# Hybrid attention and expert block: the five instruction orders written anew, and the row maxima's DMA issued by ScalarE

## The chip, the cores and the metric

One core of one Trainium2 chip. The metric is the device time of one execution in microseconds (us), lower is better. The kernel before took 746.04 us in the median of 3 runs (742.22 to 750.68).

## The reference, cut to what matters

The input is 8 sequences of 256 rows of 512 numbers in float32. Two rounds are computed on it, the second on the first one's result; each is an attention followed by an expert layer, both with a residual.

```
x = x + attention(layernorm(x))   # 32 heads of 16, 8 key/value heads, RoPE, causal softmax
x = x + experts(layernorm(x))     # dense 512x512 + bias, and the top 2 of 8 low-rank experts (rank 16)
x = x + attention_b(layernorm(x)) # same shapes, other weights
x = x + experts(layernorm(x))
```

Everything is float32 in value. The kernel makes the matrix products exact enough by splitting each operand into a high part (rounded to fp32r) and a low part (what is left), and adding three products.

## The kernel before, in words

**Stages.** A sequence in one round is a *slot* `s`; there are 16 of them, 0 to 15. A slot's attention is cut into four steps `p` = 4s to 4s+3 (64 in all) and two *halves* `h` = 2s and 2s+1 (32 in all). For a slot, TensorE (PE) runs, by the helper's name in the code:

- `tr("a")`: transposes of the normalised rows; `q01` and `q2`: projections for queries, keys and values, 8 steps each (12 and 6 matmuls a step); `vT`: transposes of the values.
- for each `p`: `A` (three pieces, all scores once, only to find each row's maximum), `M2` (transposes of those maxima), `B` (three pieces, the scores again with the maximum subtracted, through extra rows of the operand that hold the maxima), and for each half `PV` (probabilities times values, with the row sums).
- `oM`: output projection, 8 steps of 6 matmuls. Steps 0 and 1 of its four row blocks read half 2s, steps 2 and 3 read half 2s+1.
- `tr("f")`, `fA`, `fB`, `fW`, `fC`: the expert layer (router and low-rank inputs, dense product, transposes, low-rank outputs).

**The way of the maxima.** VectorE (DVE) reduces the scores (`Am`, L1094), PE transposes (`M2`, L507), ScalarE (ACT) copies them to a row tile (`mc`, to `mT`, L860), and a DMA of 8 KB (`mr`, L293) writes them into the operand tile `QK` of that step. `B` (L517) waits for it, then ACT takes the exponential (`ex`, L940), and GpSimd (POOL) masks (`causal`, L1259). There is one `mT`: `mc(p)` waits until `mr(p-1)` has landed.

**The way of the operands.** ACT copies the projections out of PSUM (`qe`, L860), SyncE (SP) swaps odd and even rows by DMA (`sw`, L270), DVE and POOL rotate (`rc`, `rs_`, `ra`), ACT and POOL split into high and low (`rh`, `kh`, `rl`, `kl`), and SP lays them out for the four steps by 12 DMAs (`st`, L282 to L287). The first rotation of the next slot (`rc`) waits until all 12 have landed. `A` of a step waits for its three.

**The way of the row sums.** After `PV(h)`: ACT copies (`oe`, L860), a DMA gathers the sums (`lc`, L299), DVE inverts (`rp`, L1123), two more transfers through DRAM spread them (`rd`, L308; `rr`, L314), `xc` (L303) moves the numerators, POOL or DVE multiplies (`mu`, L235), ACT and POOL split (`oh`, L860; `ol`, L246). Then `oM` may read.

**The way to the expert layer.** After `oM`: DVE adds the residual (`ox`, L1137), takes statistics (L1079), ACT and POOL make the scale (`eps`, L895; `power`, L1248), ACT normalises twice (`norm`, L902), PE transposes, ACT and DVE split (`high`, L860; `low`, L1064). Then `fA` may start. At the end of a slot `fx` (L1179) adds the result and SP stores it.

**Order.** Nothing chooses at run time. Each of the five engines has its own list of calls, written out in the source by a planner that ran before; the engines meet at semaphores only, and each engine works strictly in the order of its list. A step that is not ready holds up all that stands behind it on its engine, and SP's list holds all DMAs. The last argument of a PE call, as `("ex", 171)`, is the semaphore that frees its PSUM buffer.

Of the kernel before, what the change touches and what calls it, by code (L numbers as in the profile page):

```python
# [5 lines left out]
F32 = mybir.dt.float32  # L6
# [6 lines left out]
P = 128  # L13
# [42 lines left out]
def hybrid_block_kernel(nc, x_in, wqa, woa, wqb, wob, wg, wb, wl, bias_in, trig_in, krow_in, iden_in, iota_in, sums,  # L56
                        mid, out):
    with ExitStack() as ctx:
# [198 lines left out]
        def _(e):  # L257
# [146 lines left out]
            rr(27); lc(28); xc(28); st(62, 2); st(62, 0); st(62, 1); rd(28); mr(60); rr(28); st(63, 1); st(63, 0)
            st(63, 2); store(12); mr(61); lc(29); mr(62); xc(29); rd(29); rr(29); mr(63); lc(30); xc(30); rd(30)
            lc(31); rr(30); xc(31); rd(31); rr(31); store(13); store(14); store(15)
# [4 lines left out]
        def _(e):  # L411
# [175 lines left out]
            warm(5); tr("a", 0, 0); tr("a", 1, 0); q01(0, 0, 0, 1); q2(0, 0, 0, 2); q01(0, 0, 1, 1); q01(0, 1, 1, 1)  # L587
            q2(0, 0, 1, 2); q01(0, 1, 0, 1); q01(0, 2, 0, 1); q01(0, 3, 0, 1); q2(0, 1, 1, 2); q01(0, 2, 1, 1)
            q01(0, 3, 1, 1); q2(0, 1, 0, 2); q2(0, 2, 0, 2); q2(0, 3, 0, 2); q2(0, 2, 1, 2); q2(0, 3, 1, 2); vT(0, 3)
            tr("a", 2, 0, ("al", 1)); tr("a", 3, 0); q01(1, 0, 0, 1, ("rc01", 1)); q01(1, 1, 0, 1); q01(1, 2, 0, 1)  # L590
            q01(1, 3, 0, 1); q2(1, 0, 0, 2, ("rc2", 1)); q01(1, 0, 1, 1); q01(1, 1, 1, 1); q01(1, 2, 1, 1)
            q01(1, 3, 1, 1); q2(1, 1, 0, 2); q2(1, 2, 0, 2); q2(1, 3, 0, 2); q2(1, 0, 1, 2); q2(1, 1, 1, 2)
            q2(1, 2, 1, 2); q2(1, 3, 1, 2); A(0, 0, 3, ("ve", 1)); vT(1, 0, ("al", 2)); A(0, 1, 0, ("ve", 2))
            A(0, 2, 3, ("m", 1)); A(1, 0, 1, ("rc01", 2)); A(1, 1, 2, ("rc2", 2)); A(1, 2, 0, ("m", 2))
            M2(0, 3, ("m", 3)); A(2, 0, 3, ("mc", 1)); A(2, 1, 1, ("m", 4)); A(2, 2, 2, ("m", 5)); M2(1, 0, ("m", 6))
            B(0, 0, 0, ("mc", 2)); B(0, 1, 3, ("m", 7)); B(0, 2, 0, ("ex", 1)); tr("a", 4, 3, ("ex", 2))
            B(1, 0, 1, ("m", 8)); B(1, 1, 0, ("ex", 3)); M2(2, 2, ("m", 9)); B(1, 2, 1, ("ex", 4))
            A(3, 0, 2, ("mc", 3)); A(3, 1, 0, ("ex", 5)); A(3, 2, 2, ("m", 10)); B(2, 0, 1, ("ex", 6)); tr("a", 5, 3)
            A(4, 0, 0, ("m", 11)); PV(0, 1, ("ex", 7)); M2(3, 2, ("m", 12)); A(4, 1, 0, ("m", 13))
            q01(2, 0, 0, 3, ("al", 3)); q01(2, 1, 0, 3); A(4, 2, 1, ("oe", 1)); B(2, 1, 2, ("mc", 4))  # L600
            B(2, 2, 0, ("m", 14)); q01(2, 2, 0, 3); q01(2, 3, 0, 3); M2(4, 1, ("m", 15)); B(3, 0, 2, ("ex", 8))
            q01(2, 0, 1, 3); B(3, 1, 0, ("ex", 9)); B(3, 2, 1, ("mc", 5)); q01(2, 1, 1, 3); q01(2, 2, 1, 3)
# [826 lines left out]
```

## Time and profile before

| | |
|---|---|
| median of 3 runs | 746.04 us |
| the profiled execution | 747.37 us |
| its span, first to last instruction | 745.4 us |
| mean granted TensorE clock | 0.937 of full speed |
| PE busy | 662.7 us (89%) |
| DVE, ACT, POOL busy | 458.7, 433.4, 469.6 us |
| DMA | 95.14 MB, mean 128 GB/s |

PE matmuls overlap and their ends are modelled, so the busy share of PE is not its share of peak. Waits are given for the engine that waited and the one that released it. A granted clock of 0.5 is the lower of the two levels, 1.2 GHz; 1.0 is 2.4 GHz.

### The profile page before, as it was taken

Reading aid. Unit: us, or ns where it says so; the run is one execution under the profiler, and the core shown is the slowest. Engines: PE = TensorE matmul, PEld = TensorE weight load, DVE = VectorE, ACT = ScalarE, POOL = GpSimd, SP = SyncE. Lnnn points to the kernel's source line nnn. Section 1 sums busy time; section 2 is a strip of 40 time slices with the busy share of each in tenths; the row PEclk is TensorE's granted clock in tenths of the full one; section 3 lists DMA queues with packets and bytes.
Section 4 is the critical chain, followed back from the end, with each engine's and each line's share of the span. In section 5 each row is a group of like instructions: output and inputs, shape, how many; then the busy total and the mean of one; then the engine's idle time right before and its main releaser. Section 6 shows DMA issues by size and latency. Waiting matters only on the chain.

```text
span 745.4 us, 18400 instructions
## 1 busy us (share of the span) xinstructions
PE 662.7 (89%) x7498; PEld 508.1 (68%) x7498; DVE 458.7 (62%) x641; ACT 433.4 (58%) x698; POOL 469.6 (63%) x494
## 2 busy tenths in 40 slices
PE   5675989998999998998999899999999799698896
PEld 4663556876677776776777687777776687464684
DVE  2677464765576766765675765767676654664543
ACT  2535556655565766756575674848576465556531
POOL 1337295857677684957677584958676665855531
PEclk7775889999999999999999899999999899899999
DMA  9563536353464646364454626464644626264111
GB/s 324 171 192 61 115 99 150 76 140 103 100 180 100 183 103 175 99 178 136 104 176 100 203 66 153 128 130 138 137 140 106 149 76 148 90 126 108 49 37 57
DMA packets 49651, 95.14 MB, mean 128 GB/s; under 512 B 7936, under 2 KB 19840, under 8 KB 49568
## 3 DMA queue, kind: packets, MB, share of 16 engines
q1 hardware_dynamic: 49568, 93.98, 47.9%
q8 instruction: 59, 0.97, 0.5%
q14 instruction: 24, 0.20, 0.1%
HBM read 24.42 MB, written 10.49 MB: 47 GB/s over the span
## 4 chain that ended last, share of the span: by engine, by line
PE 55%; DMA 13%; SPq 11%; POOL 6%; issue 6%; ACT 5%; DVE 4%; POOLq 0%; DVEq 0%; ACTq 0%
PE PP L424 38%; PE PP L531 10%; PE PP L517 5%; DMA NR<-sums 2%; SPq L314 2%; SPq L285 2%; DMA Qs<-Qf 2%; SPq L282 2%; DMA QK<-R 2%; DMA QK<-mT 2%; ACT PT L940 2%; SPq L287 2%; PE PP L437 2%; DVE nm L1094 1%; POOL PT L1259 1%
## 5 line engine op out<-in xcount | busy, mean ns | idle before, releaser
L1094 DVE TENSOR_REDUCE nm<-PP 128x4 f32<-128x1024 f32 (+1 forms) x192 | 227.8, 1217 | 89.9 <-PE PP L424 89.3
L940 ACT ACTIVATE PT<-PP 128x1024 f32<-128x1024 f32 x192 | 191.6, 1024 | 66.9 <-PE PP L517 65.7
L1259 POOL TENSOR_SCALAR_AFFINE_SELECT PT<-PT 128x1024 f32<-128x1024 f32 x128 | 139.4, 1095 | 111.4 <-ACT PT L940 111.4
L424 PE MATMUL PP<-QK 64*128 64x128 f32 (+1 forms) x1024 | 97.0, 296 | 17.9 <-ACT PT L940 3.9
L531 PE MATMUL PP<-PT,V 128*32 128x512 f32 x768 | 95.7, 634 | 13.8 <-POOL PT L1259 11.1
L424 PE MATMUL PP<-XH,WQh 64*128 64x256 f32 x768 | 99.9, 308 | 7.9 <-DVE XL L1064 4.8
L424 PEld LDWEIGHTS PP<-QK 64*128 64x128 f32 x1024 | 83.6, 201 | 31.7 <-issue 13.7
L424 PE MATMUL PP<-XL,WQh 64*128 64x256 f32 x768 | 92.7, 290 | 0.0
L424 PE MATMUL PP<-XH,WQl 64*128 64x256 f32 x768 | 92.6, 289 | 0.0
L517 PE MATMUL PP<-QK 64*128 64x512 f32 x384 | 82.2, 435 | 10.5 <-DMA QK<-mT 5.0
L424 PEld LDWEIGHTS PP<-XH,WQh 64*128 64x128 f32 x768 | 70.4, 199 | 21.0 <-issue 12.0
L424 PEld LDWEIGHTS PP<-XL,WQh 64*128 64x128 f32 x768 | 69.2, 198 | 1.0
L204 POOL TENSOR_TENSOR Qs<-Qs,trig 128x512 f32<-128x512 f32 (+1 forms) x46 | 51.0, 1117 | 28.8 <-DMA Qs<-Qf 28.6
L424 PEld LDWEIGHTS PP<-XH,WQl 64*128 64x128 f32 x768 | 69.1, 197 | 0.0
L531 PEld LDWEIGHTS PP<-PT,V 128*32 128x32 f32 x768 | 23.2, 114 | 63.9 <-issue 50.5
L235 POOL TENSOR_TENSOR NE<-NE,NR 128x512 f32<-128x512 f32 x30 | 38.4, 1278 | 43.2 <-DMA NR<-sums 43.2
L902 ACT ACTIVATE xn<-X,nb,rs 128x512 f32<-128x512 f32 x64 | 51.9, 812 | 18.2 <-POOL nb L1250 11.4
L860 ACT ACTIVATE NE<-PP 128x1024 f32<-128x1024 f32 x32 | 32.8, 1025 | 49.8 <-PE PP L531 49.7
L424 PE MATMUL PP<-WOh,OH 64*128 64x512 f32 x256 | 56.0, 426 | 2.2 <-POOL OL L246 1.9
L424 PE MATMUL PP<-WBh,XH 64*128 64x512 f32 x256 | 55.3, 421 | 0.9 <-DVE nm L1094 0.4
L1248 POOL TENSOR_TENSOR rs<-ve,half 128x2 f32<-128x2 f32 x32 | 22.6, 707 | 51.8 <-ACT nme L896 51.6
L517 PEld LDWEIGHTS PP<-QK 64*128 64x128 f32 x384 | 38.6, 194 | 22.6 <-DMA QK<-mT 7.1
(95 smaller groups left out, 1302.7 us busy)
## 6 DMA issues: line engine op xcount, KB each, us to landing
QK<-Rh SPq DMA_DIRECT2D x64, 256.0 KB, 4.1
QK<-R SPq DMA_DIRECT2D x64, 208.0 KB, 4.1
QK<-R SPq DMA_DIRECT2D x64, 160.0 KB, 4.0
Qs<-Qf SPq DMA_DIRECT2D x32, 256.0 KB, 3.3
NR<-sums SPq DMA_DIRECT2D x64, 128.0 KB, 2.7
NE<-NE SPq DMA_DIRECT2D x32, 128.0 KB, 2.0
mid<-X SPq DMA_DIRECT2D x8, 512.0 KB, 5.0
X<-mid SPq DMA_DIRECT2D x8, 512.0 KB, 4.6
```

Of the source, the lines that this page charges most:

```text
L204: e.tensor_tensor(schunk(b), schunk(b), trigs(1, b), ALU.mult).then_inc(S[f"rs{b}"], 1)
L235: e.tensor_tensor(n, n, NR[:, :], ALU.mult).then_inc(S["mu"], 1)
L282: e.dma_start(QK[0:P:2, g, 0:1024].bitcast(F32), Rh[rows, :, :].rearrange("r c t -> r (c t)").unsqueeze(1).to_broadcast([32, 2, 1024]).bit ...
L424: ins = e.matmul(t[:, k, c], lhs(rows, which[k]), rhs(rows, which[k]), start=start, stop=stop, skip_group_check=True)
L517: ins = e.matmul(PP[t][:, a, :].rearrange("p (j q) -> p j q", j=4), keys(g, a, 4 if i == 2 else 0), x[:, :, min(i, 1), :], start=True, sto ...
L531: ins = e.matmul(PP[t][32 * c:32 * c + 32, min(i, 1), :], V[:, s % 2, i // 2, 4 * G + c, :], PT[:, (3 * p + i) % RING, 512 * a:512 * a + 5 ...
L860: return e.activation(dst, src, ACT.Copy)
L902: e.activation(xn[:, f, :], X[:, 2 * (s % XR) + i, :], ACT.Identity, bias=nb[:, f, i:i + 1], scale=rs[:, f, i:i + 1]).then_inc(S[c + "xn"], 1)
L940: e.activation(PT[:, k % RING, :].rearrange("p (a x) -> p a x", a=2), PP[t][:, :, :], ACT.Exp, scale=0.25).then_inc(S["ex"], 1)
L1094: e.tensor_reduce(o, x, AX.X, ALU.max).then_inc(S["m"], 1)
L1248: e.tensor_tensor(rs[:, f, :], ve_[:, f, :], half[:, :], ALU.pow).then_inc(S["np" + c], 1)
L1259: e.affine_select(out=blk, in_=blk, compare_op=ALU.is_ge, fill=0.0, base=0, pattern=[[0, 8], [1, 128]], channel_multiplier=-1).then_inc(S[ ...
```

## The change

It has two parts. The amount of work is the same on each engine, but for the 64 `mr` DMAs and 7 more warm-up matmuls at PE's start.

**1. `mr` is issued by ACT.** The function moves from the block of SP to that of ACT, and in ACT's list `mr(p)` always stands right behind `mc(p)`.

**2. All five lists are written anew.** In SP's list the opening loads stand in the order in which they are used (rows, then the four blocks of the first projection's weights, then the rest), where before they were mixed. In all lists the steps of attention and expert layer interleave otherwise. Which engine does a step is unchanged; the PSUM buffers are assigned anew.

```diff
             # block of SP
-            def mr(p):
-                w.wait_ge(S["mc"], p + 1)
-                e.dma_start(QK[3:P:64, p % 4, 0:1024].bitcast(F32),
-                            mT[:, :].bitcast(F32)).then_inc(S[f"md{p % 2}"], 16)
...
-            rows0(0); load(0); rows0(1); load(13); const("id"); load(6); load(14); load(5); load(16); kr(); load(7)
-            const("trig"); load(3); load(2); rows(1); rows(2); load(1); load(15); load(10); const("bias"); rows(3)
-            const("iota"); load(12); load(8); load(11); load(4); rows(4); load(9); qk(); sw(0, 0); sw(0, 2); st(0, 0)
-            st(1, 0); st(2, 0); st(3, 0); st(0, 1); st(1, 1); st(2, 1); st(0, 2); st(1, 2); st(3, 1); st(2, 2)
-            st(3, 2); sw(1, 0); sw(1, 2); wd(17); mr(0); mr(1); st(4, 0); st(4, 2); st(4, 1); mr(2); st(5, 2)
+            rows0(0); rows0(1); const("id"); load(0); load(1); load(2); load(3); const("trig"); rows(1); kr()
+            load(4); load(5); load(6); load(7); qk(); load(12); load(13); load(14); load(15); load(16); load(8)
+            load(9); load(10); load(11); rows(2); const("bias"); const("iota"); rows(3); rows(4); sw(0, 0); sw(0, 2)
+            wd(17); st(0, 0); st(1, 0); st(2, 0); st(3, 0); st(0, 2); st(1, 2); st(2, 2); st(3, 2); st(0, 1)
+            st(1, 1); st(2, 1); st(3, 1); sw(1, 0); sw(1, 2); st(4, 0); st(4, 2); st(4, 1); st(5, 1); st(5, 0)
...
             # block of PE, a slot in the middle of the run (after)
+            PV(22, 0, ("ex", 138)); B(46, 2, 2, ("ex", 139)); A(47, 1, 1, ("ex", 140)); A(47, 2, 3, ("ox", 11))
+            q01(13, 0, 0, 0, ("oe", 23)); q01(13, 1, 0, 0); q01(13, 2, 0, 0); q01(13, 3, 0, 0); M2(47, 1, ("m", 143))
+            tr("f", 20, 2, ("ex", 141)); A(48, 0, 3, ("m", 144)); A(48, 1, 1, ("mc", 48)); q01(13, 0, 1, 0)
+            q01(13, 1, 1, 0); tr("f", 21, 2); B(47, 0, 3, ("m", 145)); q01(13, 2, 1, 0); B(47, 1, 1, ("m", 146))
+            q01(13, 3, 1, 0); B(47, 2, 3, ("ex", 142)); fA(10, 0, 0, 2, ("fl", 11)); fA(10, 1, 0, 2); fA(10, 2, 0, 2)
...
             # block of ACT
+            def mr(p):
+                w.wait_ge(S["mc"], p + 1)
+                e.dma_start(QK[3:P:64, p % 4, 0:1024].bitcast(F32),
+                            mT[:, :].bitcast(F32)).then_inc(S[f"md{p % 2}"], 16)
...
             # block of POOL, opening
-            power("a", 0); power("a", 1); rs_(0, 1); ra(0, 1); ra(0, 2); rl(0, 1); kl(0); rs_(1, 0); rs_(1, 2)
+            power("a", 0); power("a", 1); ra(0, 2); rs_(0, 1); ra(0, 1); power("a", 2); kl(0); rl(0, 1)
```

## Rows read from the trace of the kernel before

**Rows 1.** The page: busy time of the engines, clock in 40 slices.

```profile
PE 662.7 (89%) x7498; PEld 508.1 (68%) x7498; DVE 458.7 (62%) x641; ACT 433.4 (58%) x698; POOL 469.6 (63%) x494
PEclk7775889999999999999999899999999899899999
```

**Rows 2.** By stretch: length, busy PE, PEld, DVE, ACT, POOL; PEclk, DMA, GB/s.

```profile
0.00:80.00 80.00, 51.71 (x482) 40.71 (x484) 45.30 (x62) 34.66 (x61) 29.89 (x35) 0.70 0.59 177
80.00:151.30 71.30, 64.34 (x740) 49.81 (x741) 41.65 (x48) 43.76 (x65) 50.33 (x49) 0.93 0.51 118
151.30:568.40 417.10, 392.25 (x4679) 304.94 (x4677) 278.42 (x388) 266.84 (x428) 296.24 (x311) 0.98 0.52 135
568.40:695.00 126.60, 110.39 (x1172) 79.67 (x1172) 71.70 (x93) 72.92 (x111) 77.95 (x80) 0.93 0.44 109
695.00:745.40 50.40, 44.03 (x444) 33.02 (x444) 21.61 (x52) 15.19 (x35) 15.19 (x22) 0.98 0.15 53
```

**Rows 3.** Chain that ended last, opening (start us, length us, what).

```profile
8.50 9.72 DMA PT<-in_wqa
...
20.13 6.86 PE PP L424 x70
...
28.65 2.43 DMA Qs<-Qf
...
35.84 0.59 SPq L282
```

**Rows 4.** Timeline, opening: first projection, next rotation, `mr` issues, first `B`.

```profile
14.79 0.58 PE L424 MATMUL PP<-XH,WQh 64*128 64x256 f32 x2 [2.47 <-DVE XL L1064]
...
51.28 1.22 DVE L1103 TENSOR_TENSOR R<-PP,trig 128x1024 f32<-128x1024 f32 x1 [2.43 <-DMA QK<-R]
...
60.13 4.85 SPq L293 DMA_DIRECT2D QK<-mT  x2
...
64.53 1.22 PE L517 MATMUL PP<-QK 64*128 64x512 f32 x4 [2.09 <-ACT mT L860]
```

**Rows 5.** `mr`: issue durations (min/median/max ns), and waits (us, times, longest).

```profile
L293 SPq DMA_DIRECT2D QK<-mT x64: 535/580/846, 60.1 to 686.1; - x64
...
PEld PP L517 <- DMA QK<-mT: 7.1, 10, 3.2
...
PE PP L517 <- DMA QK<-mT: 5.0, 6, 3.0
...
SPq L293 <- ACT mT L860: 35.7, 21, 9.4
```

**Rows 6.** Chain of waits: PE's steps at full clock (start, us, what).

```profile
261.24 0.23 PE PP L517 x2
...
263.15 0.72 PE PP L424 x12
...
707.91 3.06 PE PP L424 x24
```

**Rows 7.** Timelines of PE, POOL and DVE: half 9 in mid-run, half 31 last.

```profile
254.52 2.78 PE L531 MATMUL PP<-PT,V 128*32 128x512 f32 x24 [1.67 <-POOL PT L1259]
...
277.97 1.28 POOL L246 TENSOR_TENSOR OL<-NE,OH 128x512 fp32r<-128x512 f32 x1 [0.74 <-ACT OH L860]
...
694.96 2.78 PE L531 MATMUL PP<-PT,V 128*32 128x512 f32 x24
...
710.79 0.69 DVE L246 TENSOR_TENSOR OL<-NE,OH 128x512 fp32r<-128x512 f32 x1 [0.54 <-ACT OH L860]
```

**Rows 8.** Timeline of DVE: residual (`ox`) and low part (`low`), slot 3, slot 15.

```profile
244.16 1.22 DVE L1137 TENSOR_TENSOR X<-PP,X 128x1024 f32<-128x1024 f32 x1 [0.39 <-PE PP L424]
...
256.79 1.22 DVE L1064 TENSOR_TENSOR XL<-PP,XH 128x1024 fp32r<-128x1024 f32 x1
...
719.34 1.22 DVE L1137 TENSOR_TENSOR X<-PP,X 128x1024 f32<-128x1024 f32 x1
...
728.49 1.23 DVE L1064 TENSOR_TENSOR XL<-PP,XH 128x1024 fp32r<-128x1024 f32 x1 [0.73 <-ACT XH L860]
```

More of the change, by code:

```diff
@@ L585, in fC @@
                 ins.then_inc(S["fC"], 1)
[L587 to L600, printed above, removed]
@@ L852, in _ @@
-            fB(15, 1, 0, 0); fB(15, 2, 0, 0); fB(15, 3, 0, 0); fB(15, 0, 1, 0); fB(15, 1, 1, 0); fB(15, 2, 1, 0)
-            fB(15, 3, 1, 0); fW(15, 2, ("fl", 16)); fC(15, 1, 0); fC(15, 0, 0)
+            warm(7); tr("a", 0, 0); warm(1); tr("a", 1, 0); warm(4); q01(0, 0, 0, 1); q2(0, 0, 0, 2); q01(0, 0, 1, 1)
+            q01(0, 1, 1, 1); q01(0, 1, 0, 1); q2(0, 0, 1, 2); q2(0, 1, 1, 2); q01(0, 2, 0, 1); q01(0, 3, 0, 1)
+            q01(0, 2, 1, 1); q01(0, 3, 1, 1); tr("a", 2, 3); q2(0, 1, 0, 2); q2(0, 2, 0, 2); q2(0, 3, 0, 2)
@@ new lines, in _ @@
+            M2(0, 3, ("m", 2)); B(0, 0, 0, ("m", 3)); B(0, 1, 1, ("rc2", 2)); A(1, 0, 3, ("mc", 1))
+            A(1, 1, 2, ("rc01", 2)); A(1, 2, 0, ("ex", 1)); A(2, 0, 3, ("m", 4)); A(2, 1, 1, ("ex", 2))
+            M2(1, 2, ("m", 5)); B(0, 2, 0, ("m", 6)); A(2, 2, 2, ("mc", 2)); A(3, 0, 3, ("m", 7))
+            A(3, 1, 1, ("m", 8)); M2(2, 0, ("ex", 3)); A(3, 2, 2, ("m", 9)); B(1, 0, 0, ("mc", 3))
+            B(1, 1, 3, ("m", 10)); B(1, 2, 0, ("ex", 4)); q01(2, 0, 0, 1, ("m", 11)); q01(2, 1, 0, 1)
@@ new lines, in _ @@
+            B(7, 1, 0, ("ex", 22)); B(7, 2, 1, ("m", 25)); q01(3, 3, 1, 2); A(8, 1, 3, ("fl", 1))
+            fA(0, 0, 0, 0, ("ex", 23)); fA(0, 1, 0, 0); fA(0, 2, 0, 0); fA(0, 3, 0, 0); fA(0, 0, 1, 0)
+            fA(0, 1, 1, 0); fA(0, 2, 1, 0); fA(0, 3, 1, 0); A(8, 2, 1, ("ex", 24)); PV(3, 3, ("m", 26))
+            fB(0, 0, 0, 0, ("fg", 1)); fB(0, 1, 0, 0); fB(0, 2, 0, 0); fB(0, 3, 0, 0); M2(8, 1, ("m", 27))
+            fW(0, 3, ("oe", 4)); A(9, 0, 2, ("rc01", 4)); fB(0, 0, 1, 0); fB(0, 1, 1, 0); fB(0, 2, 1, 0)
@@ new lines, in _ @@
+            B(37, 0, 0, ("mc", 39)); B(37, 1, 2, ("m", 118)); oM(8, 2, 1, 3); oM(8, 3, 1, 3)
+            B(37, 2, 0, ("ex", 112)); A(39, 1, 1, ("al", 12)); oM(8, 2, 0, 3); oM(8, 3, 0, 3)
+            B(38, 0, 2, ("ex", 113)); B(38, 1, 0, ("ex", 114)); PV(18, 1, ("m", 119)); A(39, 2, 3, ("ox", 9))
+            B(38, 2, 2, ("ex", 115)); q01(11, 0, 0, 0, ("ex", 116)); q01(11, 1, 0, 0); M2(39, 1, ("oe", 19))
+            q01(11, 2, 0, 0); q01(11, 3, 0, 0); tr("f", 16, 3, ("m", 120)); q01(11, 0, 1, 0)
@@ new lines, in _ @@
+            M2(51, 0, ("oe", 25)); q01(14, 3, 0, 1); tr("f", 22, 2, ("m", 156)); q01(14, 0, 1, 1)
+            A(52, 0, 3, ("ex", 153)); A(52, 1, 0, ("mc", 52)); tr("f", 23, 2); q01(14, 1, 1, 1)
+            B(51, 0, 3, ("m", 157)); q01(14, 2, 1, 1); q01(14, 3, 1, 1); B(51, 1, 0, ("m", 158))
+            B(51, 2, 3, ("ex", 154)); fA(11, 0, 0, 2, ("fl", 12)); fA(11, 1, 0, 2); fA(11, 2, 0, 2); fA(11, 3, 0, 2)
+            A(52, 2, 0, ("ex", 155)); fA(11, 0, 1, 2); fA(11, 1, 1, 2); fA(11, 2, 1, 2); fA(11, 3, 1, 2)
@@ new lines, in _ @@
+            split(8); split(9); split(10); rs_(0, 0); ra(0, 0); rs_(0, 2); low("a", 1, 3); stats("a", 2); split(11)
+            stats("a", 3); stats("a", 4); rl(0, 0); low("a", 2, 0); Am(0, 0, 0); Am(0, 1, 3); Am(0, 2, 0)
+            rc(1, 2, 1); rc(1, 0, 2); Am(1, 0, 3); Am(1, 1, 2); Am(1, 2, 0); Am(2, 0, 3); Am(2, 1, 1); Am(2, 2, 2)
+            Am(3, 0, 3); Am(3, 1, 1); Am(3, 2, 2); rp(0); Am(4, 0, 0); Am(4, 1, 3); Am(4, 2, 2); Am(5, 0, 0)
+            rc(2, 0, 1); Am(5, 1, 2); rp(1); rc(2, 2, 0); Am(5, 2, 0); Am(6, 0, 2); Am(6, 1, 1); low("a", 3, 3)
```

920 lines of the change are left out of this document (451 added, 469 removed).

## The prediction

> **What bounds the kernel now.** The page first: PE is busy 662.7 us of a span of 745.4, no other engine over 63% [rows 1]. So PE sets the pace, and what a new order can win is what PE idles, 83 us, and what it runs at the lower clock. Where that lies, a table by stretch shows [rows 2]: until 80 us PE is busy 51.7 us at a granted clock of 0.70; from 80 to 151.3 (the `PV` of half 4) 64.3 of 71.3 at 0.93; the 20 halves up to 568.4 take 417.1 us, of which PE works 392.3 at 0.98, 20.9 us a half or 41.7 a slot; 568.4 to 695.0 has 110.4 of 126.6 at 0.93; the tail after the last `PV`, 44.0 of 50.4. Idle time: 28 us in the first 80, 7 in the next 71, 25 in the long middle, 16 late, 6 in the tail.
>
> The chain of waits tells what the opening waits for: a weight load of 9.7 us that ends at 18.2, half clocked PE work to 27, the swap until 31.1, rotation, then twelve `st` from 35.8 [rows 3]. The first `B` comes at 64.53, behind two `mr` issues that together held SP's queue 4.85 us [rows 4].
>
> **Part 1: `mr` on ACT.** It takes 64 issues of 0.58 us off SP, 37 us, with the 35.7 us in which SP stood at them for `mc`, and with that held up swaps, layouts and row sum transfers queued behind. It adds the 64 issues to ACT. From 0.535 (the shortest) to 0.846 us (the longest) each [rows 5] that is 34 to 54 us; I take 0.58 plus about 0.2 in which ACT waits for the end of its own copy (an estimate; the rows do not show that gap), 50 us. ACT goes from 433 to 483 us, 65% of the span, still below PE. What PE ever waited for `mT`'s transfer is 7.1 + 5.0 = 12.1 us [rows 5]: that is the upper bound of a gain. The lower bound is that all 50 us delay something PE needs: behind `mr` on ACT stand exponentials, copies for the projections, `oe` and `oh`. Each has slack of several us in most places, as ACT idled over 40%. Cover of the cost: that idle time. If it is gone, the exponentials come late, and PE's B and PV wait. I take −3 for `mr` and +3 for late ACT work, net 0, ends −12 and +51.
>
> A wait is not added beyond what was there: `mr(p)` behind `mc(p)`; `mc(p+1)` waits for the landing of `mr(p)` as before. SP's transfers and ACT's no longer pass one queue. The Trainium skill (DMA: Bandwidth & Descriptors, "Issuing engines are not separate DMA queues") says that issuing on several engines only saves the issue time; the zero above agrees. The same notes (Perfetto Trace Analysis, "DMA Instruction — HWDGE (DVE, Sync)") have the issuing sequencers share one descriptor generator with a lock wait ahead of it, which speaks against the change: ACT would stand while SP issues. No row of before shows ACT issuing, so the sum goes without it; it is a rival below.
>
> **Part 2a: the opening.** Rows and first weights now lead the queue. PE starts at 14.79 at the lower clock, and its first projection ends at 20.13 + 6.86 = 27.0 [rows 3, 4]. With the four weight blocks one behind another it should end around 22, 5 us sooner. But all of it does not carry through: the layouts need rotation, all weight splits and `wd(17)` ahead of `st`, and the remaining loads (some 8 MB) still run. So `st` starts only 0 to 1.5 us sooner than 35.84. The other gain is in PE's list: `B` of the first step now stands ahead of further `A`s, so it should come around 54 in place of 64.53, and with it exponentials, `PV` and the next projections. Not all 10.5 us count, as PE then meets less work that is ready. Seven more warm-up matmuls cost under 1 us and lie in PE's idle time before its first weights. Bounds at the `PV` of half 4 (151.3): −1.5 from `st` alone to −11 from `B` alone; I take −7.
>
> **Part 2b: the middle.** PE's work is the same: by steps of 0.72 (`q01`), 0.77 (a quarter of 3.06 for an `oM`, `fB` or `fC` step), 0.23 (`B`), 2.78 (`PV`) [rows 6, 7] a slot comes to some 36 to 37 us, against 41.7 now. A gain of up to 4 to 5 us a slot is there, if the waits go. But the new order sets two waits tighter. Counting PE work by these prices in both lists: between `PV` of the odd half and the third step of `oM` there were 21.1 us, now 15.5; from the end of `oM` to `fA` 15.0, now 11.2. What these must cover: from `PV`'s end to `ol`'s end 279.25 − 257.30 = 21.9 us in mid-run and 711.48 − 697.74 = 13.7 at the end with the queues empty [rows 7]; from `ox` to `low`, 258.0 − 244.2 = 13.9 and 729.7 − 719.3 = 10.4 [rows 8]. One slot then cannot be shorter than the first chain, 4 `oM` steps and 2 `B` (3.5), the second chain, and 8 `fA`, 2 `fB`, an `A` and a `PV` (6.5; an `fA` or `A` is 4 matmuls of 0.06, from twelve in 0.72): 24.1 + 10.0 = 34.1 with the short chains, 35.8 + 10.0 = 45.8 with the long. Even with now is at chains of 31.7. Both long chains contain POOL time that depends on the list: in half 9 `ol` alone began at 277.97, behind rotations of the next slot, and in POOL's new list `mu` of the odd half stands ahead of a rotation (`rs_`, `ra`), a `kl` and two masks that were ahead of it; SP has less in its way too. I take 29, a loop of 39, for PE a slot hardly shorter than it was once its own work and small waits are in, and +3 over the ten slots for places where a cover fails. Ends: −24 (2.4 a slot, half of what PE idles per slot, as 39.3 would be) and +41 (45.8 each slot).
>
> **Part 2c: late and tail.** 16 us idle in 126.6, at 0.93 [rows 2]: before, the last slots left PE less to mix. The new lists interleave slots 14 and 15 as the middle does; at the middle's busy share of 94%, 110.4 would take 117, −9; that is one end, +3 the other, and I take −6. In the tail PE has less work behind the last `PV` (no first half of `oM` left over) but also less filler under the 13.7 us of its chain [rows 7]; the whole tail is nearly that chain, the second one and the expert layer: −2, between −5 and +3.
>
> **Sum.** 745.4 − 7 + 0 + 3 − 6 − 2 = 733.4 us span. The profiled execution stands 2.0 over its span, at 747.4, and 1.3 above the median: 733.4 + 2.0 − 1.3 = 734.
>
> **Rivals.**
> *Nothing net (745, between 739 and 752).* The covers fail by 1 us a slot (+10), the opening gives −7 and the late stretch −3. For it: PE's idle time in the middle is only 25 us already, and every lost wait uncovers another. Against: the opening's order is a plain mistake repaired, and nothing there competes with it.
> *Slower: `ol` comes too late (762).* If POOL and ACT serve the row sums as in half 9, the loop is 45.8; if that holds in seven slots of ten, 7 × 4.1 = +29, and with −7 −6 for opening and end, the span is 761 to 762. It decides where the two chains sum to over 31.7 us; the wait is PE's third `oM` step on `OL`, and its price 45.8 − 41.7 = 4.1 a slot at most. ACT's issues make it likelier, as `oe` and `oh` lie in the first chain and two `norm`s in the second: half a us more for each of two or three `mr` passed is +1.5 a slot. Against: ACT and SP share the load better.
> *A shared issue path.* If ACT's issue has to wait until one of SP's is through, each `mr` costs ACT one SP issue more, 64 × 0.58 = 37 us [rows 5], and ACT comes to 520 us, still under PE. What of it falls in the chains above, two `mr` a slot, is 1.2 us a slot: 12 in the middle and some more around it, 747. For it: two `mr` issues of SP once took 4.85 us together [rows 4], so an issue can be held up by something. Against: the longest single one took 0.846. It is the lock wait of the Trainium skill, as above.
> *More gain (718).* The middle gives −12 and the opening −11.
> *The change does nothing in time* cannot quite be: both parts reach every list; it falls in the first rival.
>
> **Chances.** Forecast 0.5 (its own range 722 to 741), nothing net 0.19, a shared issue path 0.05, slower 0.21, more gain 0.05. Range 718 to 760: the case of more gain at the lower end, and the slower case in its milder half. A measurement of this kernel tells about 1% from no change, 738.6 to 753.5. Faster by over that: 0.52; within: 0.26; slower: 0.22.
>
> **What would show it.** The first projection over by 23 and first `B` near 54; the `PV` of half 4 near 144. If `B` comes at 60 or later, 2a is wrong. From half 4 to half 24, 417 us again within 5; if longer, PE's waits name POOL `OL` (first chain) or DVE `XL` and ACT `xn` (second), and these sums over 25 us mean the slower rival. ACT issues of `mr` at 0.6 us, and SP's waits on `mT` gone; ACT issues of over 1 us mean that SP and ACT get in each other's way. From half 24 to 31 about 120 us, and a tail of 48. What would make me wrong altogether: a queue whose turn order I misjudged, as POOL's rotation of a next slot ahead of `mu`, which repeats in every slot.

## The result and the profile after

In 20 runs each, the changed kernel took 747.13 us in the median (742.24 to 751.86) and the kernel before 744.93 us (735.53 to 751.96). The ratio is 1.0053 (95% interval 1.0029 to 1.0077): half a per cent slower, where 734 us and a gain were forecast.

The page of the changed kernel: busy times, and the clock in 40 slices. They answer to [rows 1].

```profile
PE 662.0 (89%) x7512; PEld 503.4 (67%) x7512; DVE 453.7 (61%) x641; ACT 432.0 (58%) x698; POOL 469.4 (63%) x494
...
PEclk9785999999999999999999999999999999997999
```

PE has the same busy time in the same span. The clock rose from 0.937 to 0.952 on the mean, and only its second to fourth slices and one near 680 us are low.

The table by stretch, cut at the `PV` of halves 4, 24 and 31 as in [rows 2] (the cut at 80 us is a fixed time):

```profile
0.00:80.00 80.00, 49.95 (x512) 41.06 (x516) 41.94 (x60) 35.05 (x62) 27.20 (x35) 0.77 0.66 177
80.00:153.70 73.70, 66.59 (x766) 49.91 (x758) 43.33 (x53) 45.99 (x69) 53.09 (x53) 0.98 0.50 123
153.70:575.70 422.00, 395.53 (x4686) 306.01 (x4684) 275.51 (x386) 264.62 (x427) 297.28 (x310) 0.99 0.52 133
575.70:699.30 123.60, 110.97 (x1166) 77.38 (x1166) 72.41 (x93) 73.42 (x112) 78.97 (x81) 0.93 0.44 108
699.30:746.10 46.80, 38.95 (x392) 29.04 (x392) 20.49 (x51) 12.90 (x32) 12.88 (x19) 0.97 0.15 52
```

| until | before | after | difference | forecast |
|---|---|---|---|---|
| `PV` of half 4 | 151.3 | 153.7 | +2.4 | −7 |
| half 4 to 24 | 417.1 | 422.0 | +4.9 | +3 |
| half 24 to 31 | 126.6 | 123.6 | −3.0 | −6 |
| tail | 50.4 | 46.8 | −3.6 | −2 |
| sum | 745.4 | 746.1 | +0.7 | −12 |

Of the 12.7 us between forecast and result the opening makes 9.4. Its chain of waits, beside [rows 3]:

```profile
5.26 8.72 DMA NE<-in_krow
14.00 0.77 SPq L355
14.81 0.58 SPq L329
15.44 3.86 SPq L329
19.35 3.28 SPq L329
...
28.00 0.70 SPq L270
28.74 7.08 DMA Qs<-Qf
35.84 0.70 DVE Qs L204
...
42.43 0.59 SPq L282
```

The weights were in time: PE's first projection ended at 19.5, not at 27. But SP stood until 14.0 at `qk` (L355, a broadcast of 832 KB into `QK`), because it copies what `kr` (L350, 208 KB into `NE`) brings, and `kr` landed only then. After it two single load issues took 3.86 and 3.28 us. The first swap (L270) was issued at 28.00, as before, although its data were ready at 20.5, and its transfer took 7.08 us where it took 2.43 [rows 3]. The loads that went out late were still under way then: from 28 to 30 us the DMA engines were 97% busy, before 37%. So `st` began at 42.43, in place of 35.84. These 6.6 us have two parts. The last transfer of the first swaps landed at 36.15, before at 32.20, which is 4.0 us. From there to `st`, with rotation and split between, it was 6.3 us, before 3.6: 2.6 us that lie in rotation and split, whose order on DVE and POOL is new as well. PE stood too, for 10.4 us until 38.85, at a projection of slot 1: its operand `XL` stands behind a rotation of slot 0 in DVE's list, and that rotation waited for the swap.

ACT's issue of `mr`, and who waits for `mT` (beside [rows 5]):

```profile
L923 ACTq DMA_DIRECT2D QK<-mT x64: 503/518/1122, 58.6 to 688.8; - x64
...
PEld PP L508 <- DMA QK<-mT: 10.5, 8, 2.4
...
PE PP L508 <- DMA QK<-mT: 5.9, 5, 2.2
```

An issue costs 0.52 us on ACT in the median, 33 us in all, and only one took 1.12. In the trace each begins 0.03 us behind the end of its copy, and ACT's next instruction starts at least 0.59 us behind that end.

### The profile page after: what moved, and what is told of

Read it like the earlier page. It is cut to its first block, busy times and chain, and to the rows that moved or that the text cites. A ratio compares the mean times of both kernels' runs of the same rounds, so it can differ in the third digit from the quotient of the medians.

```text
span 746.1 us, 18427 instructions
## 1 busy us (share of the span) xinstructions
PE 662.0 (89%) x7512; PEld 503.4 (67%) x7512; DVE 453.7 (61%) x641; ACT 432.0 (58%) x698; POOL 469.4 (63%) x494
## 4 chain that ended last, share of the span: by engine, by line
PE 55%; DMA 12%; SPq 8%; ACT 8%; DVE 7%; POOL 4%; issue 4%; ACTq 0%; DVEq 0%; POOLq 0%
PE PP L415 40%; PE PP L522 9%; PE PP L508 4%; DVE nm L1094 4%; DMA Lc<-NE 4%; ACT PT L935 3%; DMA Qs<-Qf 3%; SPq L282 2%; PE PP L428 2%; SPq L287 2%; SPq L329 2%; ACT NE L850 2%; DMA QK<-R 1%; SPq L285 1%; DMA NE<-in_krow 1%
## 5 line engine op out<-in xcount | busy, mean ns | idle before, releaser
L1094 DVE TENSOR_REDUCE nm<-PP 128x4 f32<-128x1024 f32 (+1 forms) x192 | 227.3, 1216 | 69.1 <-PE PP L415 68.4
L935 ACT ACTIVATE PT<-PP 128x1024 f32<-128x1024 f32 x192 | 188.1, 1025 | 61.2 <-PE PP L508 58.1
L415 PE MATMUL PP<-XH,WQh 64*128 64x256 f32 x768 | 94.9, 296 | 12.5 <-DVE XL L1064 11.0
L415 PE MATMUL PP<-QK 64*128 64x128 f32 (+1 forms) x1024 | 92.8, 295 | 11.5 <-DVE nm L1094 4.2
L415 PEld LDWEIGHTS PP<-QK 64*128 64x128 f32 x1024 | 77.7, 196 | 33.5 <-issue 17.3
L508 PE MATMUL PP<-QK 64*128 64x512 f32 x384 | 77.9, 432 | 15.4 <-DMA QK<-mT 5.9
L415 PE MATMUL PP<-XL,WQh 64*128 64x256 f32 x768 | 90.1, 283 | 0.0
L415 PE MATMUL PP<-XH,WQl 64*128 64x256 f32 x768 | 90.0, 283 | 0.0
L204 POOL TENSOR_TENSOR Qs<-Qs,trig 128x512 f32<-128x512 f32 (+1 forms) x46 | 50.9, 1108 | 33.2 <-DMA Qs<-Qf 33.1
L209 POOL TENSOR_TENSOR R<-R,Qs 128x512 f32<-128x512 f32 (+1 forms) x47 | 51.6, 1100 | 26.1 <-DVE Qs L204 21.1
L415 PEld LDWEIGHTS PP<-XL,WQh 64*128 64x128 f32 x768 | 66.3, 191 | 0.8
L1123 DVE RECIPROCAL Lc<-Lc 128x128 f32<-128x128 f32 x32 | 30.4, 950 | 51.8 <-DMA Lc<-NE 51.7
L508 PEld LDWEIGHTS PP<-QK 64*128 64x128 f32 x384 | 37.1, 190 | 31.5 <-DMA QK<-mT 10.5
```

Of the source, the lines that this page charges most:

```text
L204: e.tensor_tensor(schunk(b), schunk(b), trigs(1, b), ALU.mult).then_inc(S[f"rs{b}"], 1)
L209: e.tensor_tensor(roped(b), roped(b), schunk(b), ALU.add).then_inc(S[f"ra{b}"], 1)
L415: ins = e.matmul(t[:, k, c], lhs(rows, which[k]), rhs(rows, which[k]), start=start, stop=stop, skip_group_check=True)
L508: ins = e.matmul(PP[t][:, a, :].rearrange("p (j q) -> p j q", j=4), keys(g, a, 4 if i == 2 else 0), x[:, :, min(i, 1), :], start=True, sto ...
L935: e.activation(PT[:, k % RING, :].rearrange("p (a x) -> p a x", a=2), PP[t][:, :, :], ACT.Exp, scale=0.25).then_inc(S["ex"], 1)
L1094: e.tensor_reduce(o, x, AX.X, ALU.max).then_inc(S["m"], 1)
```

## The experiments

Twelve kernels ran, in three sets; the ratios of a set are to the kernel before, run beside them.

**1. The place of `mr`, the place of `qk`, the loads.**

`e1_mr_sp`: the new lists, `mr` back on SP.

```diff
-            mc(0, 3); mr(0); ...          # ACT
+            mc(0, 3); ...
-            sw(1, 0); sw(1, 2); st(4, 0); st(4, 2); st(4, 1); ...      # SP
+            sw(1, 0); sw(1, 2); mr(0); mr(1); st(4, 0); st(4, 2); mr(2); st(4, 1); ...
```

> The new lists, but the 64 mr go back to SP's list, each at the place in the order of start times that it had in the profiled run of the changed kernel. Theory A (mr on ACT neither costs nor gains, as I forecast; the missing gain lies in the opening): within 0.5% of the changed kernel, 743 to 751 us. Rival B (mr on ACT costs ACT time that PE then misses: 50 us in all, of which some 5 to 10 reach the end): 737 to 742. Rival C (mr on ACT is worth something, since SP's queue is full, and it hides a loss of the new order): 751 to 758.

Measured: 747.1 us, ratio 1.0015 (0.9979 to 1.0051). Theory A's range holds it. Against the 1.0053 of the changed kernel it is 0.4% less, which the intervals do not tell from nothing. The waits of PE for `mT` went up from 10.5 and 5.9 to 16.7 and 11.1 us, and the span is no longer for it (745.6 against 746.1).

`e2_mr_act`: the old lists, only `mr` moved.

```diff
-            sw(1, 0); sw(1, 2); wd(17); mr(0); mr(1); st(4, 0)         # SP
+            sw(1, 0); sw(1, 2); wd(17); st(4, 0)
-            mc(0, 3); eps("a", 3); mc(1, 0); ...                       # ACT
+            mc(0, 3); mr(0); eps("a", 3); mc(1, 0); mr(1); ...
```

> The lists of the kernel before, with only the 64 mr moved from SP's list to ACT's, each right behind its mc. Theory A: within 0.5% of the kernel before. Rival B: slower by 5 to 10 us. Rival C: faster by 3 to 7 us. The profile tells what an mr costs on ACT (0.6 us forecast) and whether ACT stands behind SP's issues (over 1 us each).

Measured: 744.4 us, ratio 0.9965 (0.9930 to 0.9999), in A's range and near the edge of C. PE's waits for `mT` almost disappear, from 7.1 and 5.0 us [rows 5]:

```profile
PEld PP L509 <- DMA QK<-mT: 1.5, 2, 0.8
...
PE PP L509 <- DMA QK<-mT: 1.1, 2, 0.6
```

`e3_qk_late`: the changed kernel, with `qk` late.

```diff
-            load(4); load(5); load(6); load(7); qk(); load(12); ...; rows(3); rows(4); sw(0, 0); sw(0, 2)
+            load(4); load(5); load(6); load(7); load(12); ...; rows(3); rows(4); sw(0, 0); qk(); sw(0, 2)
```

> The changed kernel, with one DMA moved in SP's opening: qk (832 KB to QK) from behind the eighth weight load to behind the first swap. Theory A (in the changed kernel SP waited 5.7 us for kr before qk, and qk's 10 us transfer then held the loads, so that the first swap was issued at 28.0 and landed at 35.8): the last loads land by about 20, the first swap lands by 27 to 30, st(0,0) starts at 35 to 37 in place of 42.4, the PV of half 4 comes 4 to 7 us sooner than 153.7; if the opening carries through to the end, 740 to 743 us. Rival D (what the opening wins is lost before the end, since each slot's chain sets the pace): st as much sooner, but 745 to 748 us in all. Rival E (qk's place is harmless): st(0,0) again at 41 to 43.

Measured: 743.7 us, ratio 0.9945 (0.9910 to 0.9979), 1.1% under the changed kernel's ratio, by one DMA's place in a list of 416 entries. The timeline of SP's queue:

```profile
21.23 0.56 SPq L270 DMA_DIRECT2D Qs<-Qf  x1
...
22.46 0.71 SPq L355 DMA_DIRECT2D QK<-NE  x1
24.49 0.50 SPq L270 DMA_DIRECT2D Qs<-Qf  x1
25.03 4.78 SPq L271 DMA_DIRECT2D Qs<-Qf  x1
...
38.45 3.93 SPq L282 DMA_DIRECT2D QK<-Rh  x4
```

The first swap goes out 6.8 us sooner. The second stands behind `qk`, and one of its issues takes 4.78 us. `st` starts at 38.45, the `PV` of half 4 at 147.4 in place of 153.7, and the span ends 5.6 us sooner. Theory A was right in the mechanism: the first swap landed by 27.4. `st` is 1.5 us later than its range, for the second swap, which landed at 33.2, and the median is 0.7 us above its 740 to 743. D fails: what the opening wins does reach the end.

`e4_loads`: the old lists, only the opening loads in the order of use.

```diff
-            rows0(0); load(0); rows0(1); load(13); const("id"); load(6); load(14); load(5); load(16); kr(); ...
-            ...; rows(4); load(9); qk(); sw(0, 0); sw(0, 2); st(0, 0)
+            rows0(0); rows0(1); const("id"); load(0); load(1); load(2); load(3); const("trig"); rows(1); kr(); ...
+            ...; rows(3); rows(4); qk(); sw(0, 0); sw(0, 2); st(0, 0)
```

> The kernel before, with only its opening loads put in the order of use (rows, the four blocks of the first projection's weights, then the others as in the changed kernel), qk last ahead of the first swap as it was. Theory A: q01 of slot 0 is over by 21 in place of 27.0, but the first swap still stands behind qk; it lands at 29 to 31; st(0,0) starts at 33 to 35.8, and the time is 0 to 3 us under the kernel before. Rival D: st sooner by some us and no difference in all. Rival E (loads in the order of use hold up what ACT and DVE do next): st(0,0) after 37, slower by 1 to 5 us.

Measured: 747.7 us, ratio 1.0018 (0.9981 to 1.0054). No difference in all, as D had it, but not on D's way: `st`, which D had sooner, came at 36.61, 0.8 us later than in the kernel before and between the ranges of A and E. SP's queue shows why:

```profile
15.84 0.48 SPq L340 DMA_DIRECT2D X<-in_x  x1
16.37 1.16 SPq L360 DMA_DIRECT2D QK<-NE  x1
23.20 0.54 SPq L270 DMA_DIRECT2D Qs<-Qf  x1
23.79 5.30 SPq L271 DMA_DIRECT2D Qs<-Qf  x1
...
36.61 3.90 SPq L282 DMA_DIRECT2D QK<-Rh  x4
```

The swap is issued 4.9 us sooner than in the kernel before and ends no sooner, as `qk` (here L360) is ahead of it: `qk` landed at 30.6, the swap's transfers at 30.8 and 31.9 (before 30.4 and 31.1). Sooner weights alone are worth nothing. The run also parts the two reasons for the early first projection. With the loads in order and the old warm-up it ended at 22.1, as forecast, with a granted clock of 0.50 from 10 to 18 us and 22 matmuls in 2 us from 14 to 16 and from 16 to 18. The changed kernel, with seven more warm-up matmuls, has a clock of 1.00 and 33 to 34 matmuls there, and ends it at 19.5.

**2. The opening, taken apart.**

`e5_qk_last`: `qk` behind both swaps, else the changed kernel.

```diff
-            ...; load(7); qk(); load(12); ...; rows(4); sw(0, 0); sw(0, 2)
+            ...; load(7); load(12); ...; rows(4); sw(0, 0); sw(0, 2); qk()
```

> The changed kernel with qk behind both first swaps (the run before it had qk between them, and the second swap, issued at 24.5, waited for its data until 33). Theory A (transfers pass in the order of issue, and qk's 10 us stand in the way of what comes behind): the second swap lands by 30, ra(0,2) starts by 31 in place of 33.8, st(0,0) starts at 35 to 37 in place of 38.4, and the time is 1 to 3 us under that run, 0.990 to 0.994 of the kernel before. Rival F (st must then wait for qk itself): st(0,0) at 36 or later with its wait on NE, no gain over that run.

Measured: 741.5 us, ratio 0.9948 (0.9910 to 0.9986).

```profile
24.33 0.60 SPq L271 DMA_DIRECT2D Qs<-Qf  x1
24.97 0.72 SPq L355 DMA_DIRECT2D QK<-NE  x1
...
34.79 4.00 SPq L282 DMA_DIRECT2D QK<-Rh  x4
```

The issue of 4.78 us is gone, the second swap landed at 28.5, `st` starts 3.7 us sooner, slightly sooner than theory A's range, and `PV` of half 4 is at 146.1. In time A's gain over the run before, 1 to 3 us, is missing: the ratio is the same and just outside A's 0.990 to 0.994, the profiled span, 741.7, is no shorter than the 740.5 of the run before, and the `PV` of half 8 came at 237.5 against 236.4. F's sign, `st` at 36 or later with its wait on `NE`, did not come: `st` followed the split of `Rh`, which ended at 34.70. But `qk`, for which `st` waits as well, had landed only at 34.54, so that an earlier rotation alone would win next to nothing. And the first swap took 7.0 us here too, with no `qk` ahead of it.

`e6_kr_first`: only `kr` moved forward, `qk` in its place.

```diff
-            rows0(0); rows0(1); const("id"); load(0); ...; rows(1); kr()
+            rows0(0); rows0(1); kr(); const("id"); load(0); ...; rows(1)
```

> The changed kernel with only kr moved, from the tenth to the third place of SP's list; qk stays behind the eighth weight load. It parts the two halves of the theory on the opening. If SP's wait for kr (5.7 us) was the cost, that wait is gone, the first swap is issued at 23 to 25 in place of 28.0, and 3 to 5 us are gained, 0.998 to 1.001 of the kernel before. If the transfer of qk is the cost, the loads behind it are held as before, the first swap is issued at 26 to 28, and the ratio stays at 1.003 to 1.007.

Measured: 743.2 us, ratio 1.0010 (0.9980 to 1.0039). The timeline of SP:

```profile
12.73 4.73 SPq L329 DMA_DIRECT2D PT<-in_wl  x1
17.50 3.58 SPq L329 DMA_DIRECT2D Wst<-in_wg  x4
...
23.57 1.02 SPq L270 DMA_DIRECT2D Qs<-Qf  x1
...
38.40 4.53 SPq L282 DMA_DIRECT2D QK<-Rh  x4
```

The swap is issued at 23.57, 4.4 us sooner, and the span is 3.1 us shorter; a load issue of 4.73 us behind `qk` stays. The ratio is at the upper edge of the 0.998 to 1.001 expected for the wait. So the wait for `kr` and the place of `qk` each had a share: with the wait gone the `PV` of half 4 came at 150.7, 3.0 us sooner, and with `qk` late 6.3 and 7.6 us sooner.

`e7_open`: the whole opening.

```diff
-            qe(0, 0, 1); norm("a", 3); wh(12); wh(13); wh(14); wh(15); qe(0, 2, 2)      # ACT
+            qe(0, 0, 1); norm("a", 3); qe(0, 2, 2); wh(12); wh(13); wh(14); wh(15)
-            rc(0, 0, 1); split(12); split(13); split(14); split(15); rc(0, 2, 2)        # DVE
+            rc(0, 0, 1); rc(0, 2, 2); split(12); split(13); split(14); split(15)
-            power("a", 0); power("a", 1); ra(0, 2); rs_(0, 1); ra(0, 1)                 # POOL
+            power("a", 0); power("a", 1); rs_(0, 1); ra(0, 1); ra(0, 2)
```

with SP's list as in `e5_qk_last`.

> The changed kernel with its whole opening in the order in which results are there: qk behind both swaps, on ACT the copy qe(0,2) ahead of the splits of the fourth weight group, on DVE rc(0,2) likewise, on POOL rs_(0,1) and ra(0,1) ahead of ra(0,2). Theory A: st(0,0) at 33 to 36 in place of 42.4, the PV of half 0 by 71, the end 8 to 11 us sooner than the changed kernel, 0.989 to 0.993 of the kernel before. Rival G (st needs all thirteen weight copies and qk, and these end no sooner): st(0,0) at 37 or later, 0.993 to 0.996.

Measured: 742.9 us, ratio 0.9971 (0.9936 to 1.0005). Its `st` starts at 35.59, the `PV` of half 0 at 70.3 and of half 4 at 144.4, and the profiled span is 737.5, 8.6 us under the changed kernel's. By the trace A holds. By the ratio it does not in this set: 0.9971 is above A's 0.989 to 0.993 and above G's range too. The edits on ACT, DVE and POOL are not shown to add anything to `qk`'s new place: `st` is 0.8 us later than in `e5_qk_last`, whose ratio in the same set is 0.9948. It was run once more below.

`e8_old_open`: the old lists with `mr` on ACT and this opening on SP.

```diff
-            ...; rows(4); load(9); qk(); sw(0, 0); sw(0, 2); ...; wd(17); mr(0); mr(1); st(4, 0)
+            ...; rows(3); rows(4); sw(0, 0); sw(0, 2); qk(); ...; wd(17); st(4, 0)
```

> The lists of the kernel before with mr on ACT, the opening loads in the order of use and qk behind both first swaps. It tells whether the new interleaving is worth anything beside an opening that is as good. Theory H (old and new interleaving are worth the same, the parts that count are mr on ACT and the opening): 0.991 to 0.995 of the kernel before, as the best of the new lists. Rival I (the new interleaving is better by some us up to its late stretch): 0.994 to 0.999.

Measured: 743.2 us, ratio 0.9960 (0.9922 to 0.9999). The ratio lies in I's range and just above H's, and its interval overlaps both. I does not follow from it: `e5_qk_last`, the new lists with the same place of `qk`, has 0.9948 in the same set, 0.1% less. The new interleaving is not shown to be worth anything beside the old one with an opening as good; nor is the opposite.

**3. The maxima, and `mr` once more.**

`e9_half_max_new` and `e10_half_max_old`: the maximum over half the keys, in the new and the old lists.

```diff
-                    ... rearrange("p a (j t) -> p (a j) t", j=4)
+                    ... rearrange("p a (j t) -> p (a j) t", j=4)[:, :, 0:64]
-                    ... rearrange("p a (j t) -> p a j t", j=2)
+                    ... rearrange("p a (j t) -> p a j t", j=2)[:, :, :, 0:128]
```

> The changed kernel, but DVE's maximum (Am) reads only the first half of the keys of each row block, so that each of its 192 instructions takes about 0.65 us in place of 1.22 and frees its PSUM buffer sooner; the maximum subtracted is then not the row's own. Theory J (in the middle stretch PE waits for PSUM buffers that Am, the copies and the exponentials free: by the trace 14 us ahead of A, 7 of oM, 6 of vT): DVE is 100 us less busy, waits ahead of A fall to under 8 us, PV 4 to PV 24 takes 408 to 415 in place of 422, and the kernel is 8 to 15 us faster than the changed one, 0.985 to 0.995 of the kernel before. Rival K (the waits are those of long chains, through POOL and SP, or PE's own switching between small steps): the middle stretch stays within 3 us, 1.000 to 1.006.

> The same shortening of Am in the kernel before. Theory J: as the old lists keep PE waiting longer ahead of PV (16 us in the middle) than ahead of A (6 us), the gain is less than in the new lists: 3 to 8 us, ratio 0.989 to 0.996. Rival K: within 0.3% of the kernel before. If both kernels gain over 10 us alike, DVE's share in the chain of the maxima is what counts, in either interleaving.

Measured: 740.8 us, ratio 0.9907 (0.9871 to 0.9944), and 744.1 us, ratio 0.9964 (0.9927 to 1.0001). The first ratio lies where J had it, the second just above J's 0.989 to 0.996 and just outside K's 0.3%, and J is wrong all the same. The maximum subtracted is then not the row's own. The groups of instructions tell that the edit did what it should in the new lists (192 maxima of 684 ns, where they took 1216):

```profile
L1094 DVE TENSOR_REDUCE nm<-PP 128x4 f32<-128x512 f32 (+1 forms) x192 | 126.9, 684 | 104.3 <-PE PP L415 103.7
```

But the table by stretch, from half 4 to 24, to 31 and to the end:

```profile
151.40:574.70 423.30, 395.90 (x4686) 306.53 (x4684) 213.93 (x386) 263.94 (x427) 296.92 (x309) 0.98 0.52 133
574.70:691.50 116.80, 104.99 (x1166) 74.30 (x1166) 53.29 (x93) 73.08 (x112) 78.89 (x82) 0.99 0.46 114
691.50:738.40 46.90, 38.93 (x392) 28.94 (x392) 20.57 (x51) 12.99 (x32) 12.97 (x20) 1.00 0.15 52
```

In the middle DVE works 62 us less (213.93 against 275.51) and the stretch takes 423.3 us, as it took 422.0. Of the fall in the waits ahead of `A` that J wanted nothing is seen: 15 us, as 14 before (how they are summed stands in the next section). The maxima do not hold PE there, as K had it. The gain lies in the late stretch, 116.8 against 123.6, and 2.3 us of it in the opening. What happens there is in the changed kernel's chain of waits:

```profile
670.38 5.03 PE PP L522 x24
...
681.17 1.24 DVE nm L1094
682.71 0.28 ACT mT L850
683.03 0.50 PE PP L508 x2
683.58 0.52 PE PP L415 x4
684.12 1.23 DVE nm L1094
685.40 0.81 PE PP L415 x4
686.24 1.23 DVE nm L1094
687.79 4.84 PE PP L522 x24
```

The maxima of the last slot stand in the path one by one, with little other work left for PE, and both `PV`s here take about 5 us in place of the 2.78 that one takes at full clock [rows 7]. By stretches of 5 us, with PE's busy time first and the granted clock third from the end:

```profile
665.00:670.00 5.00, 3.42 (x30) 2.31 (x28) 5.00 (x6) 2.88 (x4) 3.08 (x3) 0.81 0.65 132
670.00:675.00 5.00, 4.62 (x24) 1.12 (x24) 3.00 (x3) 0.87 (x2) 2.27 (x2) 0.51 0.87 204
```

So PE worked 3.4 of 5 us, then had the lower clock for this `PV`; ahead of the second one it worked 3.3 of 5 us (680 to 685), and the clock was 0.51 again. The traces of `e1_mr_sp`, `e11_open_mr_sp` and `e12_open_again`, all with the new order, have these two `PV`s (halves 29 and 30) at 4.3 to 5.1 us, and those of the kernel before and of `e10_half_max_old` at 2.78: this loss of some 4 us came with the new order. With the shorter maxima the first takes 2.78 and the second 3.92, which is 3 us of the 6.8 gained in this stretch; no slice of the page after the middle is under 0.9. In the old lists the same edit left the stretches at 421.9 and 126.6 us, so there it gained nothing that the table shows; the profiled execution is the longest of its twelve (749.7 us).

`e11_open_mr_sp` and `e12_open_again`: the kernel with the whole opening in order, with `mr` on SP (at the places of `e1_mr_sp`), and just as it was.

```diff
-            mc(0, 3); mr(0); ...                                        # ACT
+            mc(0, 3); ...
-            ...; sw(0, 0); sw(0, 2); qk(); ...; sw(1, 2); st(4, 0)      # SP
+            ...; sw(0, 0); sw(0, 2); qk(); ...; sw(1, 2); mr(0); mr(1); st(4, 0)
```

> The run with the whole opening in order (label e7_open), but mr back on SP. With mr on SP the changed kernel measured 1.0015 and with mr on ACT 1.0053; in the old lists it was 1 and 0.9965: opposite signs, both near the measurement's limit. If the place of mr is worth nothing in the new lists, this is within 0.4% of the same kernel with mr on ACT in this set; if ACT's 33 us of issues cost something there, it is 3 to 5 us faster (0.4 to 0.7% under it); if it helps as in the old lists, 2 to 4 us slower.

> The kernel with the whole opening in order a second time, as the partner of the run with mr on SP, on the same chip. Its first set gave 0.9971 (0.9936 to 1.0005) with a profile whose span was 8.6 us under the changed kernel's. If that span is what it is worth, the ratio is 0.990 to 0.995; if the first ratio is, 0.995 to 0.999.

Measured: 741.1 us, ratio 0.9959 (0.9924 to 0.9995), and 740.1 us, ratio 0.9903 (0.9862 to 0.9945). The second set of the opening bears out its span (735.5 here), with a ratio in the range that was expected if the span is what it is worth. With the first, 0.9971, the mean is 0.994; the two intervals meet between 0.9936 and 0.9945. Its table by stretch:

```profile
0.00:80.00 80.00, 56.64 (x608) 46.50 (x608) 44.84 (x63) 40.84 (x68) 32.36 (x38) 0.81 0.69 186
80.00:146.40 66.40, 59.49 (x662) 43.75 (x662) 40.53 (x51) 39.46 (x63) 48.79 (x48) 0.97 0.48 126
146.40:567.50 421.10, 395.00 (x4686) 305.45 (x4684) 275.45 (x386) 264.81 (x427) 297.02 (x310) 0.99 0.52 133
567.50:688.80 121.30, 109.27 (x1166) 76.38 (x1167) 72.56 (x93) 73.69 (x112) 79.12 (x82) 0.94 0.45 110
688.80:735.50 46.70, 38.90 (x392) 28.98 (x392) 20.43 (x51) 12.84 (x32) 12.83 (x19) 1.00 0.14 52
```

All stages behind the `PV` of half 4 are within 2.3 us of the changed kernel's; that `PV` of half 4 is 7.2 us sooner. `mr` on SP is 0.56% slower than on ACT here, by ratios whose intervals overlap by a little, although its profiled span (735.3) is as short. Within the span two differences cancel, and the same two are there between `e1_mr_sp` and the changed kernel: with `mr` on SP the middle is shorter (417.4 and 419.2 us against 421.1 and 422.0) and the late stretch longer (125.3 and 125.6 against 121.3 and 123.6). These are single traces, so it is a hint that ACT's issues cost something in the middle, not a proof.

## Why the prediction was wrong

**The opening: the step that failed.** It read: "`st` starts only 0 to 1.5 us sooner than 35.84", and took 7 us of gain at the `PV` of half 4. `st` started 6.6 us later, and the `PV` of half 4 came 2.4 us later. I had counted the loads and their order, but not `qk`. `kr` is the tenth entry in both lists, but `qk`, before behind all the loads, now stands five entries behind `kr` and ahead of nine of the 17 weight loads. It waits for `kr` (5.7 us with SP idle, where before SP did not stand there at all), and while `qk` is under way one or two of the next issues take 3 to 5 us. So loads and swaps go out late, and the swap meets loads that are still under way. `e6_kr_first` shows the first share, `e3_qk_late` and `e5_qk_last` the two together. Of the 6.6 us at `st` that leaves 2.6 behind the swaps' landing, in the order of the rotations; `e7_open`, which puts that order right too, was no faster there, and what it would be worth is not shown. With the opening repaired the `PV` of half 4 came at 146.1, 144.4 and 146.5 (`e5_qk_last`, `e7_open`, `e12_open_again`), 5 to 7 us under the kernel before, so the forecast's 7 was the most that there was. The other reason that I gave, `B` of the first step ahead of further `A`s, held as a distance: it came 6.7 us behind the first `A`, against 18.1 us before. But the first `A` itself was 7.4 us late, at 53.8, and so `B` came at 60.5, past the 60 that I had named as the sign that this part is wrong. With the opening repaired it came at 53.9, where I had written 54.

**`mr` on ACT: right in size.** Forecast 0 with ends −12 and +51. Three comparisons give, for ACT against SP, −0.35% (old lists), +0.4% (new lists) and −0.56% (new lists with the opening in order), each at the limit of what was measured. ACT's price was 0.59 us from the end of a copy to its next instruction, under the 0.78 taken. The rival of a shared issue path is not borne out: of the 64 issues on ACT in the changed kernel, the 32 that overlap an issue of SP took 0.51 to 0.53 us like the others, and the one of 1.12 overlaps none. So the lock wait of the Trainium skill (Perfetto Trace Analysis, "DMA Instruction — HWDGE (DVE, Sync)") is not visible as a price here. What the prediction gave in favour of this rival was misread: the 4.85 us of two `mr` issues [rows 4] are 0.67 us at 60.13 and 0.57 us at 64.41, and between them SP stood for the copy into `mT`, which ended at 64.38. The long issues of this case, 3.86, 3.28, 4.73, 4.78 and 5.30 us, are SP's own, each while `qk` was under way.

**The middle: right in sign, +4.9 against +3.** But the reason was not mine. The chain from `PV` to `ol` shrank as hoped, in half 9 from 21.9 us to 15.7 (`PV` from 257.75 for 2.78 us, then):

```profile
274.96 1.28 POOL L246 TENSOR_TENSOR OL<-NE,OH 128x512 fp32r<-128x512 f32 x1 [2.01 <-ACT OH L850]
```

From `ox` to `low` it is some 12.5 us. These sum to 28, close to the 29 taken, and below the 31.7 from which the slower rival would decide; that rival is refuted, as PE has no wait for `OL` in the changed kernel's trace. A slot took 42.2 us all the same. I took for each PE step of this stretch the time from its start to the next step's, less what such a step takes at full clock, and summed it by the step that came next: waits ahead of `PV` fell from 16 to 7 us, ahead of `q2` from 8 to 2, ahead of `tr` from 8 to 5, and those ahead of `A` rose from 6 to 14, of `oM` from 3 to 7, of `vT` from under 1 to 6. Removed waits came back as many small ones. The half maxima show that the length of DVE's maxima is not the cause. What it is stays open. Two single traces with `mr` on SP had a middle shorter by 3 to 4 us, as said above. The bound of −24 was called half of what PE idles; by [rows 2] PE idled 25 us in this stretch, so it is nearly all of it.

**The late stretch and the tail: −6.6 in place of −8.** The sum is near, but by luck: the late stretch gave 3.0 of the 6, the tail 3.6 where 2 was taken. The late stretch is held by the last slot's maxima and by the clock, which was at the lower level for two `PV`s after PE had worked 3.4 and 3.3 of 5 us; I had put it down to missing work to mix, and had no term for the clock.

**The sum.** The likeliest case failed mainly by one term, the opening; of the rivals, "nothing net" gave 745 with the right sum for a wrong reason: it had the opening still giving −7. The point that I called against it, that nothing competes with the opening's repaired order, was the error itself.

## What to carry to other kernels

Where a queue's list is reordered, read it from the first entry as its engine does, and look for the entry that waits for another's landing and for the one with many bytes. In this kernel "loads in the order of use" were worth nothing until the first dependent transfer, the swap, had no such entry in front of it. Compare orders by the step that releases the first stage, not by when its inputs arrive. And before a wait is counted as a gain in the middle of a kernel whose main engine is 94% busy, ask which small waits will take its place.

The best version measured is the changed kernel with its opening in order (`e7_open`, `e12_open_again`): ratios 0.9971 and 0.9903 to the kernel before, so some 0.6% faster than it and 1.2% than the changed kernel. Moving `qk` alone gave 0.9945 and 0.9948, which is not told apart from it. The half maxima do not count here, as they compute something else.

## What the runs showed of the hardware

A broadcast DMA of 832 KB took 9.8 us from issue to landing in the changed kernel. From 16 to 22 us, with it under way, the 16 engines were over 90% busy but moved 100 to 183 GB/s, against 390 to 404 with the plain loads from 6 to 10 us. It also writes only 32 partitions; which of the two makes it slow no run shows.

While it was under way one or two of the next issues on SP took 3.3 to 5.3 us each, in the changed kernel, `e3_qk_late`, `e4_loads` and `e6_kr_first` alike. In these four traces no other issue of SP took over 2.6 us.

A swap took 2.4 us in the kernel before, where the engines were 37% busy around it (28 to 30 us), and 7.1 us in the changed kernel, where they were 97% busy. The broadcast had landed by then, at 23.8, and in `e6_kr_first`, where a swap took 7.2 us, at 19.9, which is 3.6 us before the swaps. What was under way beside them were the loads that it had held up.

An issue on ACT took 0.52 us, whether SP was issuing at the same time or not.
